# First weight group loaded and summed in two halves; the step lists of all five queues rearranged

## The reference

```python
def xattn(h, adj_raw, Wq, Wk, gamma_raw):          # h: 4 x 512 x 128, adj_raw: layernorm(x)
    sim = einsum('bhnd,bhmd->bnm', Q, K) / (sqrt(32) * 4)
    threshold = top_k(sim, 153)[0][:, :, -1:]
    A = sigmoid(sim) * (sim >= threshold)
    A = (A + swapaxes(A, -1, -2)) * 0.5
    return (1 - gamma) * adj_raw + gamma * A       # gamma = sigmoid(gamma_raw)
def bitlinear(x, w):                               # act_quant: 127 / row maximum, rounded
    return act_quant(rmsnorm(x)) @ weight_quant(w).T   # w: scale 1 / mean(|w|), to -1, 0, 1
def ffn(x):                                        # w_gate, w_up: 2048 x 512; w_down: 512 x 2048
    return bitlinear(silu(bitlinear(x, w_gate)) * bitlinear(x, w_up), w_down)
x = x + xattn(ctx, layernorm(x), Wq, Wk, gamma_raw)
x = x + ffn(layernorm(x))
```

## Time and profile before

| what | value |
| --- | --- |
| median of 3 runs | 271.9 us (271.83 to 272.65) |
| the profiled execution | 272.7 us |
| its span, first to last instruction | 269.8 us |
| busy share PE / DVE / ACT / POOL | 80 / 80 / 71 / 63 % |
| mean granted clock of PE | 0.911 of full |
| DMA | 39.18 MB, mean 145 GB/s |

### The profile page before, as it was taken

One profiled execution on the slowest core, in us unless ns is written; L12 is line 12 of the kernel. 1 busy time (PEld: TensorE's weight loads), 2 busy tenths in 40 slices (PEclk: granted clock), 3 DMA queues, 4 the chain that ended last, 5 costly groups with the idle time before them and its releaser, 6 DMA issues.

```text
span 269.8 us, 3680 instructions
## 1 busy us (share of the span) xinstructions
PE 215.5 (80%) x947; PEld 105.0 (39%) x958; DVE 215.6 (80%) x379; ACT 192.0 (71%) x325; POOL 171.2 (63%) x324
## 2 busy tenths in 40 slices
PE   7744501503986896799999999999999999999985
PEld 7212101402733352343445444444544444444432
DVE  0368987998879998997999899897988787488381
ACT  2488995999999999998988967663619185241420
POOL 2045798885886868788977778886661823408330
PEclk9965755565799999999999999999999999999999
DMA  4999999979849478364104044306096115190675
GB/s 129 392 348 386 388 327 188 420 187 214 151 81 161 78 88 157 69 117 90 31 1 79 2 78 88 88 0 101 10 244 140 39 36 140 19 197 12 125 201 206
DMA packets 78998, 39.18 MB, mean 145 GB/s; under 512 B 67968, under 2 KB 70272, under 8 KB 78464
## 3 DMA queue, kind: packets, MB, share of 16 engines
q1 hardware_dynamic: 78976, 38.94, 58.6%
HBM read 17.96 MB, written 4.19 MB: 82 GB/s over the span
## 4 chain that ended last, share of the span: by engine, by line
PE 31%; ACT 20%; issue 15%; DVE 15%; POOLq 6%; POOL 6%; DMA 4%; DVEq 3%; ACTq 0%
PE U L394 10%; PE DN L413 10%; PE G L380 9%; ACT junk_c L491 6%; ACT S L540 5%; DVE S L741 4%; DMA S<-S 3%; ACT WdT L533 3%; DVE amh L746 2%; DVE m L607 2%; ACT sg L516 2%; ACT junk_x L505 1%; PE TR L413 1%; POOLq L911 1%; POOL X L935 1%
## 5 line engine op out<-in xcount | busy, mean ns | idle before, releaser
L380 PE MATMUL G<-WgT,xqT 128*128 128x512 bf16 x256 | 60.5, 379 | 4.7 <-ACT sg L516 4.6
L516 ACT ACTIVATE sg<-G,gsc 128x1024 f32<-128x1024 f32 x32 | 35.6, 1112 | 40.2 <-PE G L380 36.1
L394 PE MATMUL U<-WuT,xqT 128*128 128x512 bf16 x256 | 60.5, 379 | 1.7 <-DVE S L741 1.2
L491 ACT ACTIVATE junk_c<-rows,srch 128x512 int8<-128x512 f32 (+1 forms) x72 | 51.1, 716 | 5.0 <-POOL srch L904 3.3
L741 DVE TENSOR_TENSOR S<-U,sg 128x1024 f32<-128x1024 f32 x32 | 39.0, 1218 | 14.2 <-PE U L394 11.6
L1000 POOL TENSOR_SCALAR S<-S,qh 128x2048 int16<-128x2048 f32 x15 | 31.1, 2076 | 24.7 <-DVE qh L790 23.0
L413 PE MATMUL DN<-WdT,S 128*128 128x512 bf16 x198 | 45.7, 379 | 0.5
L380 PEld LDWEIGHTS G<-WgT,xqT 128*128 128x128 bf16 x256 | 24.5, 98 | 36.4 <-issue 5.5
L394 PEld LDWEIGHTS U<-WuT,xqT 128*128 128x128 bf16 x256 | 24.5, 98 | 33.7 <-DVE S L741 5.0
L746 DVE TENSOR_REDUCE amh<-S 128x1 f32<-128x2048 f32 x15 | 34.0, 2270 | 0.1
L524 ACT ACTIVATE junk_h<-S 128x2048 int8<-128x2048 f32 x16 | 30.5, 1903 | 3.7 <-DVE S L741 3.6
(11 more groups left out here) (144 smaller groups left out, 376.8 us busy)
## 6 DMA issues: line engine op xcount, KB each, us to landing
S<-in_L_ffn_w_gate SPq DMA_DIRECT2D x4, 1024.0 KB, 9.2
X<-in_x SPq DMA_DIRECT2D x4, 1024.0 KB, 10.5
S<-in_L_ffn_w_up SPq DMA_DIRECT2D x4, 1024.0 KB, 14.7
S<-in_L_ffn_w_down SPq DMA_DIRECT2D x4, 1024.0 KB, 6.4
out<-X SPq DMA_DIRECT2D x16, 256.0 KB, 2.8
C<-in_ctx SPq DMA_DIRECT2D x2, 256.0 KB, 6.7
C<-in_ctx SPq DMA_DIRECT2D x1, 512.0 KB, 11.0
S<-S SPq DMA_TRANSPOSE x17, 4.3
```

Of the source, the lines that this page charges most:

```text
L380: last = nc.tensor.matmul(G[:, c * 512:(c + 1) * 512], xqT[:, t, k, :], WgT[:, 4 * n:4 * n + 4, k, :], start=(k == 0), stop=(k == KD - 1))
L394: last = nc.tensor.matmul(U[:, c * 512:(c + 1) * 512], xqT[:, t, k, :], WuT[:, 4 * n:4 * n + 4, k, :], start=(k == 0), stop=(k == KD - 1))
L491: A(junk_c[:, j, :].bitcast(U8) if r == ROUNDS else junk_c[:, j, :], ROWS[a % 2][:, j, :], ACT.Sign, bias=nthr[:, j:j + 1], accum_out=cs[: ...
L516: A(sg[:, u % 2, :], G[:, :], ACT.Silu, scale=gsc[:, b % 2, t:t + 1]).then_inc(silu_done, 1)
```

## The change

Group 0 of w_gate is loaded by two DMAs of 512 KB (w_load_half), each with a semaphore of its own, and its |w| is summed on DVE by two steps (w_abs_half) into columns 0 and 4 of a sum tile that is one column wider; w_total(0) and w_scale(0) take five columns instead of four. Apart from that, the lists of SP, PE, ACT, DVE and POOL hold the same calls as before in another order. Of the lists, the first lines are shown, and in full where the text below follows them:

```diff
@@ sums
-        wsum = sb("wsum", [P, 3, 4])
+        wsum = sb("wsum", [P, 3, 5])
+        s_wh = [sem(f"s_wh{h}") for h in range(2)]
-        n_dve = [4 * (w + 1) - n_act[w] for w in range(3)]
+        n_dve = [4 * (w + 1) + 1 - n_act[w] for w in range(3)]
+        N_SUMS = (5, 4, 4)
+            def w_load_half(w, h):
+                sp.dma_start(STAGE[w][:, h * GROUP // 2:(h + 1) * GROUP // 2].rearrange("p (c d) -> p c d", d=D),
+                             w_gate[h * 256:(h + 1) * 256, :].rearrange("(c p) d -> p c d", p=P)).then_inc(s_wh[h], 16)
-                nc.tensor.matmul(DN[:, 0:4], onesf[:, :], wsum[:, w, :], start=True, stop=True).then_inc(s_wtot, 1)
+                nc.tensor.matmul(DN[:, 0:N_SUMS[w]], onesf[:, :], wsum[:, w, 0:N_SUMS[w]], start=True,
+                                 stop=True).then_inc(s_wtot, 1)
+            def w_abs_half(w, h):
+                dve.wait_ge(s_wh[h], 16)
+                V.tensor_reduce(wsum[:, w, 4 * h:4 * h + 1], STAGE[w][:, h * GROUP // 2:(h + 1) * GROUP // 2], AX.X,
+                                ALU.add, apply_absolute_value=True).then_inc(s_wabs_dve, 1)
@@ SP
-            w_load(0, w_gate, 0); w_load(0, w_gate, 1); w_load(0, w_gate, 2); c_load(0, 1, 2); c_load(1, 2, 4)
-            w_load(0, w_gate, 3); x_load(0); x_load(1); w_load(1, w_up, 0); w_load(1, w_up, 1); w_load(1, w_up, 2)
-            x_load(2); w_load(1, w_up, 3); w_transpose(0, 0); w_transpose(0, 1); w_transpose(0, 2)
-            w_load(2, w_down, 0); w_load(2, w_down, 1); w_load(2, w_down, 2); w_load(2, w_down, 3)
-            w_transpose(0, 3); w_transpose(1, 0); x_load(3); xq(0, 0); w_transpose(1, 1); xq(0, 1); xq(0, 2)
-            w_transpose(1, 2); w_transpose(1, 3); xq(0, 3); w_transpose(2, 0); w_transpose(2, 1)
+            w_load_half(0, 0); w_load_half(0, 1); w_load(0, w_gate, 1); x_load(0); c_load(0, 1, 2)
+            w_load(0, w_gate, 2); w_load(0, w_gate, 3); w_load(1, w_up, 0); w_load(1, w_up, 1); w_load(1, w_up, 2)
+            w_load(1, w_up, 3); c_load(1, 2, 4); w_transpose(0, 0); w_transpose(0, 1); w_load(2, w_down, 0)
+            w_load(2, w_down, 1); x_load(1); w_load(2, w_down, 2); w_load(2, w_down, 3); w_transpose(0, 2)
+            w_transpose(0, 3); w_transpose(1, 0); w_transpose(1, 1); xq(0, 0); x_load(2); w_transpose(1, 2)
+            w_transpose(1, 3); xq(0, 1); xq(0, 2); xq(0, 3); w_transpose(2, 0); w_transpose(2, 1)
...
@@ PE
-            sims(1, 0); sims(1, 1); sims(1, 2); sims(1, 3); w_total(1); miss_total(0); a_transposes(0, 0)
-            a_transposes(0, 1); a_transposes(0, 2); a_transposes(0, 3); pre(2); pre_g(2); warm(8, 0); sims(2, 0)
-            warm(8, 1); gate(0); up(0); miss_total(1); sims(2, 1); w_total(2); sims(2, 2); gate(1); sims(2, 3)
-            a_transposes(1, 0); a_transposes(1, 1); up(1); gate(2); up(2); gate(3); up(3); a_transposes(1, 2)
-            a_transposes(1, 3); gate(4); up(4); gate(5); pre(3); up(5); gate(6); up(6); down(0, 0); down(0, 1)
-            gate(7); pre_g(3); up(7); sims(3, 0); gate(8); miss_total(2); sims(3, 1); up(8); sims(3, 2); gate(9)
-            sims(3, 3); up(9); down(1, 0); gate(10); up(10); gate(11); down(1, 1); a_transposes(2, 0)
+            sims(1, 0); sims(1, 1); sims(1, 2); w_total(1); sims(1, 3); miss_total(0); a_transposes(0, 0)
+            a_transposes(0, 1); a_transposes(0, 2); a_transposes(0, 3); pre(2); pre_g(2); warm(8, 0); warm(8, 1)
+            sims(2, 0); gate(0); miss_total(1); sims(2, 1); w_total(2); sims(2, 2); up(0); gate(1); sims(2, 3)
+            up(1); a_transposes(1, 0); gate(2); up(2); a_transposes(1, 1); gate(3); a_transposes(1, 2)
+            a_transposes(1, 3); gate(4); up(3); up(4); gate(5); up(5); gate(6); pre(3); up(6); down(0, 0)
+            down(0, 1); gate(7); up(7); pre_g(3); sims(3, 0); gate(8); miss_total(2); sims(3, 1); up(8); gate(9)
+            sims(3, 2); up(9); sims(3, 3); gate(10); up(10); down(1, 0); gate(11); down(1, 1); a_transposes(2, 0)
...
@@ ACT
-            counts(0, 0, 0); counts(0, 0, 1); counts(0, 1, 0); counts(0, 1, 1); counts(0, 2, 0); evac_GT(1)
-            counts(0, 2, 1); sims(1, 0); counts(0, 3, 0); counts(0, 3, 1); tanhs(0, 0); tanhs(0, 1); sims(1, 1)
-            w_abs(1, 0); w_abs(1, 1); sims(1, 2); sims(1, 3); tanhs(0, 2); w_abs(1, 2); tanhs(0, 3); w_abs(1, 3)
-            counts(1, 0, 0); counts(1, 0, 1); counts(1, 1, 0); w_round(1, 0); counts(1, 1, 1); counts(1, 2, 0)
+            counts(0, 0, 0); counts(0, 0, 1); counts(0, 1, 0); counts(0, 1, 1); counts(0, 2, 0); counts(0, 2, 1)
+            counts(0, 3, 0); evac_GT(1); counts(0, 3, 1); tanhs(0, 0); tanhs(0, 1); tanhs(0, 2); w_abs(1, 0)
+            sims(1, 0); w_abs(1, 1); w_abs(1, 2); w_abs(1, 3); tanhs(0, 3); sims(1, 1); sims(1, 2); sims(1, 3)
+            w_round(1, 0); counts(1, 0, 0); counts(1, 0, 1); w_round(1, 1); counts(1, 1, 0); counts(1, 1, 1)
...
@@ DVE
-            w_abs(0, 0); sim_stats(0, 0, 1); sim_stats(0, 2, 3); w_abs(0, 2); w_abs(0, 3); x_stats(0, 0, 1)
-            w_scale(0); w_quant(0, 0); w_quant(0, 1); w_quant(0, 2); x_stats(0, 2, 3); rank(0, 0); rank(0, 1)
-            rank(0, 2); rank(0, 3); sim_stats(1, 0, 1); sim_stats(1, 2, 3); note_misses(0); threshold(0)
-            general_path(0); w_scale(1); masked(0, 0); masked(0, 1); masked(0, 2); masked(0, 3); x_stats(1, 0, 1)
...
-            note_misses(2); h_cast(2); mul(7); x_cast(1, 2, 3); sim_stats(3, 0, 1); threshold(2); general_path(2)
-            masked(2, 0); mul(8); final(0); masked(2, 1); masked(2, 2); mul(9); sim_stats(3, 2, 3); h_absmax(3)
...
-            general_path(3); masked(3, 0); masked(3, 1); mul(19); masked(3, 2); final(5); masked(3, 3)
-            h_absmax(8); h_cast(7); x1(3, 0); h_floor(2); h_scale(8); h_absmax(9); h_scale(9); final(6); h_cast(8)
-            mul(20); x1(3, 1); x1(3, 2); final(7); h_cast(9); x1(3, 3); x_absmax(3, 0); x_absmax(3, 1); mul(21)
+            w_abs_half(0, 0); w_abs_half(0, 1); sim_stats(0, 0, 1); sim_stats(0, 2, 3); x_stats(0, 0, 1)
+            w_abs(0, 2); w_abs(0, 3); x_stats(0, 2, 3); w_scale(0); w_quant(0, 0); w_quant(0, 1); w_quant(0, 2)
+            rank(0, 0); rank(0, 1); rank(0, 2); rank(0, 3); sim_stats(1, 0, 1); w_scale(1); sim_stats(1, 2, 3)
+            note_misses(0); threshold(0); w_quant(0, 3); general_path(0); masked(0, 0); masked(0, 1); masked(0, 2)
...
+            mul(7); threshold(2); h_scale(2); x_cast(1, 2, 3); h_absmax(3); mul(8); final(0); general_path(2)
+            h_scale(3); mul(9); sim_stats(3, 0, 1); sim_stats(3, 2, 3); masked(2, 0); masked(2, 1); masked(2, 2)
+            masked(2, 3); x_stats(3, 0, 1); h_cast(2); mul(10); final(1); x1(2, 0); x_stats(3, 2, 3); h_cast(3)
...
+            x_cast(2, 2, 3); final(4); h_absmax(8); h_cast(6); mul(18); h_floor(2); rank(3, 3); note_misses(3)
+            h_scale(8); h_cast(7); final(5); mul(19); threshold(3); general_path(3); masked(3, 0); masked(3, 1)
+            mul(20); masked(3, 2); masked(3, 3); final(6); h_cast(8); mul(21); h_absmax(9); h_scale(9); x1(3, 0)
...
@@ POOL
-            sigmoids(1, 1); sigmoids(1, 2); sigmoids(1, 3); first_threshold(2, 0); first_threshold(2, 1)
-            add_a(1, 0); add_a(1, 1); add_a(1, 2); d_coef(0); update(2, 0, 0); update(2, 0, 1); update(2, 1, 0)
-            add_a(1, 3); update(2, 1, 1); update(2, 2, 0); h_round(0); h_round(1); update(2, 2, 1); ln_coef(2)
+            sigmoids(1, 1); sigmoids(1, 2); sigmoids(1, 3); d_coef(0); add_a(1, 0); add_a(1, 1); add_a(1, 2)
+            first_threshold(2, 0); first_threshold(2, 1); update(2, 0, 0); add_a(1, 3); h_round(0)
+            update(2, 0, 1); update(2, 1, 0); update(2, 1, 1); update(2, 2, 0); update(2, 2, 1); ln_coef(2)
+            h_round(1); update(2, 3, 0); x_round(1, 0); x_round(1, 1); x_round(1, 2); x_round(1, 3)
...
```

142 lines of the change are left out of this document (70 added, 72 removed).

## The result

The changed kernel takes 275.34 us (median of 8, 273.1 to 277.79), the kernel before, timed beside it, 272.75 (271.83 to 273.82): ratio 1.0085, 95% interval 1.0058 to 1.0111. (Ratios leave out executions in the slow state, here the one of 277.79.) It is slower by about 2.6 us, where the prediction had it faster; 275.34 also lies above the range. The profiled execution took 275.45 us with a span of 273.7; in before they were 272.7 and 269.8. So the spans are 3.9 apart and the medians 2.6: what lies around the span was 1.75 us here and 2.9 there, and differed by as much between executions.

A forecast was written before the change was run, and what follows sets the result against it. Bound: how early ACT and DVE bring PE to its dense stretch, and whether DVE keeps up. Span 269.8 - 1.4 = 268.4, 271.3 profiled, 270.5 median (chance 0.48); case range 269.4 to 271.2, whole range 268.8 to 273.6.

The forecast's parts named there:

- Halved load: First weight load and its sum on DVE, ahead of 14.09 us: landing half sooner moves nothing behind, zero.
- Up to the first quantising: Front with x_load(0) moved ahead: w_quant(0,0) 1 to 1.5 us later, rank(0,0) where it was, zero on the chain.
- ACT's idle time: ACT's 3.4 us idle before counts(1,0,0): w_round(1,0) fills it, -1.9 us, bounds 0 and -2.4.
- Up to the dense stretch: From silu(0) to mul(8): mul(0) at 83.7, mul(8) at 126.9 instead of 129.43, -2.5 us.
- the lead of 2.5 us: At mul(8), ahead of PE's dense stretch: 1.9 from ACT's idle, 1.0 from DVE's order, less 0.4 of new waits.
- the walk: Hand-following all five new lists with row durations, each step starting when its engine and waits allow; mul(9) at 130.4.
- Inside the dense stretch: mul(9) to mul(19): DVE +1.8 us, about 2 of waits half swallowed, mul(19) 1.5 earlier, capping PE's 1.7 lead.
- PE idle by more than 2 us between 131 and 250: Sign in the dense stretch that the profile would show at once if the prediction were wrong.
- The rival of the clock: After gate(0), a 2.3 us gap drops PE to 1.2 GHz, mul(0) 1.7 late: 272.2, no change; chance 0.14.
- The slower rival: DVE's extra 1.8 us without the lead: mul(9) at 132.7, mul(19) at 189.2, up(20) waits, 273.7; chance 0.25.
- The end of 14.9 us: Last stretch from the end of up(31), one row's chain to down(15): order kept, the 14.9 us stay.
- the carrying over: Going from span to median: 2.9 us around the span, median 0.8 below the profiled run.

The follow-up runs named there:

- a_silu_fill9: Changed kernel with silu(13) right behind counts(3,2,0) on ACT and 9 filler matmuls ahead of up(1) on PE: 273.55 us, ratio 1.0053.
- a_warm: Changed kernel plus 16 filler matmuls on PE ahead of up(1), no list changed: 274.92 us, ratio 1.0101.
- a_silu_warm: Changed kernel with silu(13) right behind counts(3,2,0) on ACT and 16 filler matmuls ahead of up(1): 274.64 us, ratio 1.0090.
- b_half: Kernel before with only the first weight load in two halves and its absolute sums apart: 272.16 us against 272.5, ratio 0.9987.
- b_front_fill9: Kernel before with w_scale(1) behind sim_stats(1,0,1), w_round(1,0) ahead of counts(1,0,0), and 9 filler matmuls ahead of gate(6): 272.25 us, ratio 0.9988.
- a_mul0: Changed kernel with mul(0) on DVE moved ahead, to right behind masked(1,1): 275.94 us, ratio 1.0124.
- a_silu: Changed kernel with only silu(13) moved on ACT, to right behind counts(3,2,0): 275.25 us, ratio 1.0090.
- b_fill9: Kernel before plus 9 filler matmuls on PE ahead of gate(6): 271.67 us, ratio 0.9977.
- a_pool: Changed kernel with POOL's sequence 3 reordered: first thresholds ahead of h_round(3), update steps ahead of add_a steps: 275.36 us, ratio 1.0108.
- a_sp: Changed kernel with only hT_rows(1) moved on SP, to right behind hT_rows(0): 274.25 us, ratio 1.0051.
- a_fix: Changed kernel with silu(13) behind counts(3,2,0), sims(3,3) ahead of up(9), DVE's x_absmax/x_scale(2) behind mul(13), x_cast(2,0,1) behind mul(14): 276.77 us, ratio 1.0138.
- h_ab: Changed kernel's lists up to up(8), silu(8), mul(8), sigmoids(2,3), x_load(3), remaining steps in the order of before: 276.58 us, ratio 1.0140.

## Why the prediction was wrong

**The account.** With the clock held, 273.55 - 271.67 = 1.9 us are the new orders' own loss. The rest of each median is put down to the clock: 275.34 - 273.55 = 1.8 in the changed kernel, 272.75 - 271.67 = 1.1 in before, 0.7 between them. Together 2.6. These medians are of different groups, between which before itself moved from 272.19 to 272.75, so the shares are good to about half a microsecond. (silu(13), which a_silu_fill9 moves, is worth nearly nothing by itself: the profiles of a_warm and a_silu_warm differ by 0.33 us at mul(31), 0.19 of which was there at mul(8).) Of the 1.9, 0.9 are hT_rows(1) and DVE's steps at mul(13), measured; the last 1.0 are waits at up(9) and gate(16), read from a profile.

**Halved load: 0.** Right (b_half).

**Up to the first quantising: 0 on the chain, w_quant(0,0) 1 to 1.5 later.** Right on the chain; w_quant(0,0) came 0.4 later (24.98 against 24.57) and rank(0,0) at 31.41, as walked (31.5).

**ACT's idle time: -1.9. This is the step that failed.** The filler was there, and ACT reached silu(0) 0.94 us earlier, with 1.26 us given back to the late second thresholds. But the sum carried ACT's gain through to mul(8). In before silu(0) ends at 81.6, and mul(0) on DVE starts at

```profile
83.05 1.19 DVE L741 TENSOR_TENSOR S<-U,sg 128x1024 f32<-128x1024 f32 x1
```

without a wait: 1.4 us of slack, in which DVE was at its own work. The prediction itself said of mul(0) and mul(6) that they hang "on DVE's own work", and still booked 1.9 us from ACT. A gain on the engine that is full doesn't count where the hand-over to the next engine already has slack; the two moved steps alone cost 0.3 to 0.6 us in b_front_fill9 (there ACT gained only 0.33 at silu(0), so it is the sign that this run shows, and not the price of a filled gap).

**Up to the dense stretch: mul(0) 83.7, mul(8) 126.9; the lead of 2.5 us was 0.1.** The whole error is there at mul(0) and stays the same: mul(0) came at 86.04, mul(5) at 108.54 instead of 106.2, mul(6) at 115.05 instead of 112.9, mul(7) at 124.09 instead of 121.8, mul(8) at 129.34, each 2.2 to 2.4 us behind the walk. Of the 2.3 at mul(0), 1.1 are masked(1,3), which took 1.79 us where a row of before has 0.7; and DVE reached masked(1,0) only at 81.18 (80.14 in before), since w_scale(2) now stands ahead of it and began at 80.44. The walk counted which steps stand ahead and used lengths taken where no other engine disturbed them. It is DVE's work up to mul(1) that counts and not the place of mul(0): in a_mul0 that came at 82.50 and mul(1) still at 90.57, where the changed kernel has 89.45.

**Inside the dense stretch: DVE +1.8.** The size of the extra work was right; that a fuller queue would swallow half of 2 us of waits was not. In a_silu's profile, with no fall in it, mul(9) to mul(19) take 56.6 us (132.96 to 189.52) against 54.7, and the walk had 55.5 in its middle. So mul(19) came 2.1 us later than in before instead of 1.5 earlier: 2.6 of the 3.6 stood at mul(9) already, 1.0 came here. But up(20) didn't wait for mul(19) in any kernel with the changed rear: PE had paid before, ahead of up(9), up(13) and up(14). What was left out is POOL: its queue from h_round(2) to h_round(4) moved by up to 13 us and was walked only as far as h_round(1). "PE idle by more than 2 us between 131 and 250" was named as a sign, with no cause for it, and it came true. (The sum takes 1.4 where the paragraph has 1.5, and the range ends at 271.2 where a lead of 0.5 gives 271.4; nothing hangs on either.)

**The rival of the clock (0.14).** Its mechanism is the one that was seen, at another place: not after gate(0), where PE stood 0.87 us instead of 2.3 and up(0) kept its 1.89, but behind the gaps ahead of up(1) and gate(14). Its price was 1.7 and measured 1.5 to 1.8. The prediction ruled it down by one row, the gap of 2.29 us at 109.49 with the clock at 1.00. That row is one execution; b_fill9, which fills this very gap, narrows before's executions from 2.3 to 0.3 us. The Trainium skill (TensorE: Matmul & The Clock Gate, section "Why this matters for your kernels") warns that idle gaps between bursts of matmuls put PE back to half rate, but names longer gaps than these. The traces here show falls behind gaps of 1.99 to 2.29 us as well, in a part of the executions.

**The slower rival (0.25).** Its sign was right, its mul(9) where it was (132.96) and its mul(19) at 189.2 nearly so (189.52 in a_silu), and its 273.7 lies beside the undisturbed level of 273.55. Only the place where PE pays was another: not a wait at up(20), but those at up(9), up(13) and up(14). The clock's part of the median it didn't have.

**The end of 14.9 us and the carrying over.** The end held. Taking 0.8 us between profile and median as fixed was not safe: b_fill9 has before's span within 0.1 us (269.9) and takes 271.67 in its profiled execution, where before's took 272.7.

## What to carry over

Before adding up a gain along a path, look at each hand-over for the slack that already stands there: only the engine that ends last passes a gain on, and here that was DVE and then POOL, not the full ACT. An error at the first hand-over is carried whole to the last: compare walk and profile step by step, and ask where the difference first appears. Walk every queue of a rearranged kernel to the end, the least busy one too. And where PE has gaps of about 2 us between bursts, one profile that shows the clock at 1.00 is one draw: look at the spread of the single times, and a few filler matmuls that fit the gap show what part of the spread goes with it.

## What the runs showed of the hardware

The same gap ahead of up(1), 2.26 to 2.29 us behind the same work, left the granted clock at 1.00 in four profiled executions (after, a_silu, a_pool, a_sp: up(1) 1.90 us) and was followed by 0.50 in two (a_fix 3.38, h_ab 3.40). The gap of 2.3 us ahead of gate(6) left it at 1.00 in all four profiles that have it. The fall doesn't come in the gap but up to about 1 us into the work behind it. With 9 float32 matmuls of 128x128 (2.17 us) in the gap, the 11 or 12 executions of each of six kernels lay within 0.6 us. In the profiles one fall costs 1.5 to 1.8 us, much of what a whole rearrangement moved. masked(1,3) on DVE, half of whose pairs in the earlier trace rows is 0.7 us, took 1.79 us at 84.33, without a wait, and 1.80 in a_silu_fill9; in a_mul0 it was masked(1,2) instead, 1.84 at 83.64. Each time POOL's add_a(1,0) ran beside it (84.30, 1.27 us, in the changed kernel); beside POOL's sigmoids in before such a step took 0.75. What lengthened it no run tells apart. hT_rows(1) stood 11.2 us in SP's queue behind three transposes that waited for their input.
